# A mixture-of-experts kernel's drain: expert block 0 ahead of group 14's choice of experts, group 15's choice behind block 1

## What is computed

```python
x = x + elu(softmax(masked leaky_relu(e_src + e_dst)) @ (layernorm(x) @ W))
xn = layernorm(x)
gate_scores = xn @ Wg.T + bg                      # 8 experts
topk_scores, topk_idx = top_k(gate_scores, 2)
topk_probs = softmax(topk_scores)
for e in range(8):
    h = relu(xn @ W1[e].T + b1[e])                # 128 -> 512
    y = h @ W2[e].T + b2[e]                       # 512 -> 128
    out += combine[..., e] * y
x = x + out
```

## Time and profile before

| what | value |
|---|---|
| median of 3 runs | 443.16 us (442.94 to 443.46) |
| the profiled execution's own time | 443.27 us |
| its span, first to last instruction | 441.5 us |
| PE busy | 406.2 us (92%), 2272 instructions |
| DVE busy | 359.7 us (81%), 1410 instructions |
| ACT busy | 321.0 us (73%) |
| POOL busy | 285.4 us (65%) |
| chain that ended last | PE 64%, DVE 20%, ACT 5%, DMA 4%, issue 4% |
| mean granted clock of TensorE | 0.988 |

### The profile page before, as it was taken

The page is one execution under the profiler, slowest core; times in us unless marked ns, Lnnn a source line. Parts: engine busy times, 40 slices in busy tenths (PEclk is TensorE's granted clock), DMA queues, the critical chain, the costliest instruction groups (busy, mean ns, idle before and its releaser), DMA issues.

```text
span 441.5 us, 9161 instructions
## 1 busy us (share of the span) xinstructions
PE 406.2 (92%) x2272; PEld 308.4 (70%) x2290; DVE 359.7 (81%) x1410; ACT 321.0 (73%) x760; POOL 285.4 (65%) x292
## 2 busy tenths in 40 slices
PE   7998888889998888999999999999999999999960
PEld 3656666666666666688888888888888887878520
DVE  5689999999998898999888888778778777766772
ACT  2678888888888988689888777767867877877400
POOL 1041777777777777677777777667666666766651
PEclk9999999999999999999999999999999999999995
DMA  6996344333333344443533333233233223297799
GB/s 170 266 381 235 98 122 120 110 97 104 104 97 104 103 121 121 128 138 106 192 102 102 122 96 116 94 84 91 90 89 90 74 76 90 89 320 239 243 291 297
DMA packets 56292, 63.04 MB, mean 143 GB/s; under 512 B 7744, under 2 KB 40896, under 8 KB 56000
## 3 DMA queue, kind: packets, MB, share of 16 engines
q1 hardware_dynamic: 36592, 34.88, 26.8%
q0 software_dynamic: 9344, 20.10, 13.5%
q10 hardware_dynamic: 10320, 7.66, 6.0%
HBM read 27.28 MB, written 26.94 MB: 123 GB/s over the span
## 4 chain that ended last, share of the span: by engine, by line
PE 64%; DVE 20%; ACT 5%; DMA 4%; issue 4%; SPq 1%; POOL 1%; DVEq 0%; ACTq 0%; POOLq 0%
PE bank L1441 7%; PE bank L1455 7%; PE bank L1454 7%; PE bank L1457 7%; PE bank L1445 7%; PE bank L1442 7%; PE bank L1425 3%; PE bank L1433 3%; PE bank L1403 3%; PE bank L1316 3%; DVE xn L1066 3%; PE bank L1401 3%; DVE bn L901 2%; DVE score L1043 2%; DVE neg_max L1048 2%
## 5 line engine op out<-in xcount | busy, mean ns | idle before, releaser
L520 POOL DMA_INDIRECT expert_slots<-rows,slot_i x128 | 124.5, 973 | 53.7 <-issue 34.5
L712 ACT ACTIVATE yb<-bank,b_sb 128x512 f32<-128x512 f32 x36 | 24.8, 688 | 50.9 <-PE bank L1457 50.9
L1454 PE MATMUL bank<-hh,w_hi 128*128 128x512 f32 x144 | 60.0, 417 | 0.0
L1441 PE MATMUL bank<-xh,w_hi 128*128 128x512 f32 x144 | 58.5, 406 | 0.8 <-ACT xh L697 0.5
L1455 PE MATMUL bank<-hh,w_lo 128*128 128x512 f32 x144 | 57.4, 398 | 0.0
L1445 PE MATMUL bank<-xl,w_hi 128*128 128x512 f32 x144 | 56.9, 395 | 0.2 <-DVE xl L1122 0.2
L1442 PE MATMUL bank<-xh,w_lo 128*128 128x512 f32 x144 | 56.8, 395 | 0.0
L1457 PE MATMUL bank<-hl,w_hi 128*128 128x512 f32 x144 | 56.6, 393 | 0.0
L536 POOL DMA_INDIRECT moe_rows<-hexp,ysi x40 | 41.2, 1029 | 18.7 <-issue 9.8
L536 POOL DMA_INDIRECT moe_rows<-hrelu,ysi x40 | 41.2, 1031 | 17.5 <-issue 10.2
L1146 DVE CAST hh<-z 128x512 fp32r<-128x512 f32 x36 | 16.7, 464 | 42.6 <-ACT z L702 42.4
(11 more groups left out here) (166 smaller groups left out, 1049.6 us busy)
## 6 DMA issues: line engine op xcount, KB each, us to landing
rows<-xn SPq DMA_DIRECT2D x32, 256.0 KB
xs<-expert_slots SPq DMA_DIRECT2D x27, 260.0 KB
x_all<-x SPq DMA_DIRECT2D x16, 256.0 KB, 3.9
w_raw<-w_t SPq DMA_DIRECT2D x2, 2048.0 KB, 12.4
w_raw<-moe_rows SPq DMA_DIRECT2D x16, 256.0 KB, 4.0
out<-x_all ACTq DMA_DIRECT2D x16, 256.0 KB, 6.0
xs<-expert_slots ACTq DMA_DIRECT2D x11, 260.0 KB
w_hi<-moe_rows SPq DMA_DIRECT2D x9, 256.0 KB, 4.3
```

What stands on the lines that cost most here:

```text
L520: nc.gpsimd.indirect_dma_start(out=slots, out_offset=bass.IndirectOffsetOnAxis(ap=slot_i[q][:, k * SUB + j:k * SUB + j + 1], axis=0), in_= ...
L712: nc.scalar.activation(yb[:, :], ps_y[:, :], ACT.Identity, bias=b2_sb[:, e:e + 1]).then_inc(yb_ok, 1)
L1441: nc.tensor.matmul(ps_h[c][:, :], w1_hi[:, e, chunk], xh[:, :], start=True, stop=False)
L1454: nc.tensor.matmul(ps_y[:, :], w2_hi[:, e, c, :], hh[:, c, :], start=c == 0, stop=False)
```

## The change

In ACT's drain `gap_exp(14)` and `gap_exp(15)` move behind block 0's and block 1's `result`, and `turned_norm(15)` moves behind chunk 1 of block 1. In DVE's drain the second norm of group 15 and all halves of block 0 come ahead of `choose(14)`; the weights, counts and slots of group 14 come behind halve(1, 0); the whole choice of group 15, counts included, comes behind block 1's halves, low_x(2) and weigh(0). In PE's drain the second layer of block 0 runs through without fills; `rank(14)` moves into block 1's first layer, `norm_turns(15)` too, `gates(15)` behind `transpose_x(2)`, and `rank(15)` into block 2, behind its first layer; for that, blocks 2 and 3 are written out in place of the loop.

```diff
 ACT drain
                 second_root(last)
                 hidden(0, 0, 2)
-                gap_exp(last - 1)
                 hidden(0, 0, 3)
                 round_x(1)
                 load_block(act, sure_row(2), 2)
                 second_norm(last, 1)
-                turned_norm(last)
                 result(0, 0)
+                gap_exp(last - 1)
                 hidden(1, 0, 0)
                 hidden(1, 0, 1)
-                gap_exp(last)
+                turned_norm(last)
                 hidden(1, 0, 2)
                 hidden(1, 0, 3)
                 round_x(2)
                 load_block(act, sure_row(3), 3)
                 result(1, 0)
+                gap_exp(last)
 DVE drain
                 halve(0, 0)
-                choose(last - 1)
-                choose_both(last - 1)
+                newton_1(last)
                 halve(0, 1)
-                newton_1(last)
                 newton_2(last)
                 newton_3(last)
                 second_shift(last)
+                halve(0, 2)
+                halve(0, 3)
+                low_x(1)
+                choose(last - 1)
+                choose_both(last - 1)
+                halve(1, 0)
                 gap_sum(last - 1)
                 first_weight(last - 1, q, m)
                 second_weight(last - 1, q)
                 row_ids(last - 1, q)
-                halve(0, 2)
                 add_counts(last - 1)
                 add_bases(last - 1)
                 write_slots(last - 1, 1 - q, (t + 1) // 2)
-                halve(0, 3)
-                low_x(1)
-                next_tokens(last)
-                choose(last)
-                choose_both(last)
-                halve(1, 0)
-                gap_sum(last)
                 halve(1, 1)
-                add_counts(last)
-                add_bases(last)
                 halve(1, 2)
                 halve(1, 3)
                 low_x(2)
                 weigh(0, 0, 0)
+                next_tokens(last)
+                choose(last)
+                choose_both(last)
+                gap_sum(last)
+                add_counts(last)
+                add_bases(last)
                 first_weight(last, 1 - q, (t + 1) // 2)
 PE drain
                 transpose_x(1)
-                result(0, 0, 0)
-                fill(ps_h[0], FILL_DRAIN + 2)
+                for c in range(HC):
+                    result(0, 0, c)
+                hidden(1, 0, 0)
+                hidden(1, 0, 1)
+                norm_turns(last, 1)
+                hidden(1, 0, 2)
                 rank(last - 1)
-                result(0, 0, 1)
-                fill(ps_h[0], FILL_DRAIN)
-                norm_turns(last, 1, ps_h[0])
-                result(0, 0, 2)
+                hidden(1, 0, 3)
+                transpose_x(2)
                 pe.wait_ge(count_ok, last)
                 gates(last, ps_gate_late)
-                result(0, 0, 3)
-                for c in range(HC):
-                    hidden(1, 0, c)
-                rank(last)
-                transpose_x(2)
                 transpose_y(0)
                 for c in range(HC):
                     result(1, 0, c)
 PE, blocks 2 and 3
                 pe.wait_ge(lo_ok, e + 1)
+                if e == 1:
+                    for i in range(2 * e, 2 * e + 2):
+                        for c in range(HC):
+                            hidden(i, e, c)
+                        if i == 2:
+                            rank(GROUPS - 1)
+                        transpose_x(i + 1)
+                        transpose_y(i - 1)
+                        for c in range(HC):
+                            result(i, e, c)
+                    continue
                 with pe.Fori(2 * e, 2 * e + 2) as i:
                     expert_block(i, e)
```

## The result

The changed kernel takes 443.95 us (median of 21 executions, 442.13 to 446.10), the kernel before 442.79 beside it (21 executions, 441.83 to 444.38). The ratio is 1.0028, its 95% interval [1.0017, 1.0039]: 0.28% or 1.2 us slower where 0.3 us faster was forecast. The profiled execution has an own time of 444.28 us and a span of 442.5.

A forecast was written before the change was run, and what follows sets the result against it. PE and DVE were taken as near their limit in the drain, PE with slack in fills. 2.9 us ahead, less 2.0, 0.2 and 0.4, gave 0.3 us faster: 442.9 us, range 441.8 to 443.9.

The forecast's parts named there:

- The sum of the drain: From block 0's second layer to block 3's start: PE's lead less what is given back, 0.3 us faster.
- 2.9 ahead: PE begins block 2's first layer at 189.2 instead of 192.14, 2.9 us earlier.
- 2.0 of it given back in the wait: Ahead of block 2's second layer PE waits some 2 us for DVE's first high part.
- 0.2 to the rank that moved here: In block 2, rank(15) behind the first layer costs PE 0.2 us.
- 0.4 to a second layer paced by DVE: Block 2's second layer runs at DVE's pace, which costs 0.4 us.
- Nothing of it reaches the path: POOL, held some 0.3 us by group 14's later slots, delays nothing; block 8's load comes ten microseconds later.
- within half a microsecond of 207.3: POOL's scatters should end within this distance of their earlier end at about 207.3.
- Behind that nothing gives or takes: After block 3's start no further gain or loss: halve(3, 0) comes at about 200.4, wanted at 201.9.
- The rival of the clock: PE's clock falls in the wait before block 2's second layer: 2.4 us longer, 445.3 us; chance 0.07.
- by that rule this rival would be the forecast: By the skill's rule that idle gaps drop PE's clock, the fall in block 2's wait would be forecast.
- the upper end: DVE never waits for rank(15) before block 2's halves: 1.4 us faster, 441.8 us; chance of over 0.2% faster 0.22.
- The edit only swaps one wait for another: Block 2's new wait takes all of PE's lead: 443.2 to 443.8 us; chance 0.06 of going past no change.

The follow-up runs named there:

- the repeat: The changed kernel run once more, unaltered: 444.14 us, ratio 1.0015 to the kernel before.
- sep_after: The changed kernel with blocks 0 to 3 weighed into four buffers of their own: 443.52 us, ratio 1.0013 to the kernel before.
- long_wait: The changed kernel with three useless 128x512 additions on DVE ahead of block 2's halves: 447.17 us, ratio 1.0087 to the kernel before.
- sep_halves: The changed kernel with block 2's halves moved ahead on DVE and four own buffers for blocks 0 to 3: 442.00 us, ratio 0.9973 to the kernel before.
- after: The changed kernel itself, unaltered, in its first run against the kernel before: 443.95 us, ratio 1.0028.
- fill_wait: The changed kernel with 8 fills on PE in the wait ahead of block 2's second layer: 443.97 us, ratio 1.0012 to the kernel before.

## Why the prediction was wrong, point by point

**The sum of the drain** was "2.9 ahead, 2.0 of it given back in the wait, 0.2 to the rank that moved here, 0.4 to a second layer paced by DVE". The trace has 2.64 ahead (192.14 before, 189.67 less 0.17 after), 1.56 in the wait, 0.51 between the two (189.67 to 193.76 is 4.09 us, 3.58 before: the rank, and the tail of the last transposes that nothing follows at once), and 0.66 for the paced layer (195.32 to 198.86 is 3.54, not 2.88). So 0.1 slower, not 0.3 faster: each term is right within 0.45 us. A wait was overlooked, too: group 15's gates on PE need the counts of group 14, which DVE now writes at 185.28, and PE comes to them a little before; some 0.4 us lie between its transposes and the gates (184.58 to 185.49, of which 0.3 show as idle). It is most of what is missing from the first term. The drain's sum alone would thus have given no change; the rest of the loss lies outside it.

**"Nothing of it reaches the path"** is the step that failed. It looked at when group 14's slots are ready (0.3 us of delay forecast; none in the first profile, 0.5 in the repeat) and at the first load at block 8 that waits for all scatters. It left out that POOL's queue holds block 0's scatter behind group 15's rows, and that block 4 reuses block 0's buffer. `weigh` of block 4 ran at 217.36 before; by the semaphore events in the traces the scatter that frees its buffer had landed at 214.81 there, and lands at 220.57 here. Of these 5.8 us, 1.5 are lateness that POOL had ahead of the changed stretch, 2.75 come up between group 13 and block 0's scatter, and 1.5 in the scatter itself (8.7 us from its first start to its landing, 7.2 before), which nothing here explains. POOL's last slots were to be sent "within half a microsecond of 207.3"; they end at 211.52, 4 us later, and 2.7 later in the repeat. "Behind that nothing gives or takes" fell with it: 1.27 us at block 6 in the first profile. That the buffer costs time is shown in the order with block 2's halves first: with the buffers apart 0.9973 [0.9960, 0.9985], sharing them 1.0011 [1.0001, 1.0022], the rest alike. For the order of the change itself the trace shows it in one of two profiles, and no pair of runs tells it from the noise.

**The rival of the clock** got 0.07 because the earlier trace rows show idle times of about 2 us without a fall. That reading was right for two profiles of the changed kernel (1.56 and 1.52 us, clock 1.00) and wrong as a bound: after 1.85 us in sep_after and 3.37 in long_wait it fell. Its price was put at 2.4 us for block 2's second layer and measured 1.1 and 1.2, since DVE paces that layer anyway and the clock was back ahead of its end. Idle times before a fall and without one lie side by side here (1.85 and 1.84 us), so the earlier trace rows could not exclude it. The Trainium skill, "TensorE: Matmul & The Clock Gate", in its section on HAM oscillation, has waits between bursts of matmuls bring the lower clock; here that holds in some executions of the same order of work. The waits of its example are longer than this one, so the prediction's "by that rule this rival would be the forecast" reads more into it than it states. In the unaltered change neither of the two profiles shows a fall; the mean clocks point to one in at least a quarter of its executions.

**The other rivals.** DVE did wait for the rank (1.21 us; 1.1 in the repeat), so the upper end, 441.8, needed another order; sep_halves is such an order, with free buffers, and gives 442.00, 1.3 us under the kernel before beside it. "The edit only swaps one wait for another" is what the drain shows by itself. Of the 1.16 us between the medians the traces show two causes, the buffer and the clock, either of which takes 1.1 to 1.4 us of an execution that it strikes. How the loss of the unaltered kernel divides between them stays open, since the intervals of after, sep_after and fill_wait overlap, and some 0.1% isn't explained by either. Whether 443.95 lies just above or just below 443.9 is chance; that it lies above the kernel before is not, by the interval of the 21 executions.

## What to carry to other kernels

Follow each queue from the moved work to the next use of every buffer it frees: an engine with a backlog and 34% idle time can still be the one that sets when a buffer comes free, 20 us later. Count what runs beside a queue-fed engine, not its own instructions only: in one execution the same 24 transfers cost 2.75 us more, as they met more of another engine's two-input subtractions. Look at more than one execution, too: POOL came to group 13 with a difference of 1.4 us in two of the same kernel, and the buffer was late enough to cost anything in one of them only. And where an edit takes filling work out ahead of a wait, the clock has to be priced from the wait's own length, by a run with the wait filled and one with it lengthened.

## What the runs showed of the hardware that was not expected

- A POOL transfer that starts 0.05 to 0.2 us behind the start of a 128x512 DVE instruction with two SBUF inputs takes 1.36 to 1.53 us in place of 0.96. One that starts 0.25 to 0.45 us behind takes 1.07 to 1.25. Start and duration together make 1.51 to 1.53 us in 73 of 74 cases, so the hold ends at one point of the DVE instruction, some 0.14 us ahead of its end. That was read from the two traces; no run took the subtractions away.
- The clock fell behind 1.85 us of idle PE in one execution and not behind 1.5 to 1.6 us in two others; a fall cost 1.1 to 1.2 us, not the double time of the layer, which DVE paced in part.
- Between the first and the second transfer of group 14, POOL stands idle for 1.63 us ("issue"; 1.85 before); the other profiles have 1.5 to 2.6 us there. Nothing in the traces explains it, and it wasn't tried.
